# Attention scores turned onto the key side, with the row maximum entered as a contraction row and the sums formed by additions in PSUM

## The reference

```
xr   = x.reshape(B, C, S).transpose(0, 2, 1)
qkv  = (xr @ w_qkv + b_qkv).reshape(B, S, 8, 192);  q, k, v = split(qkv, 3)
attn = softmax(einsum('bihd,bjhd->bijh', q, k) * 64**-0.5, axis=2)
out  = einsum('bijh,bjhd->bihd', attn, v).reshape(B, S, 512) @ w_proj + b_proj
return out.transpose(0, 2, 1).reshape(x.shape) + x
```

## Time and profile before

| | us |
|---|---|
| median of 3 runs | 4386.79 (4386.68 to 4387.8) |
| span of the profiled execution | 4385.1 |
| TensorE busy, share | 4312.1, 98% |
| VectorE | 3439.8, 78% |
| ScalarE | 3020.3, 69% |
| GpSimd | 2179.6, 50% |

### The profile page before, as it was taken

How to read it: one execution, slowest core, us unless ns; L and a number is a source line. 1 busy time by engine, 2 the same in 40 slices (tenths; PEclk the granted TensorE clock), 3 DMA queues, 4 the chain that set the end, 5 groups by cost and what they waited for, 6 DMA issues and landing times.

```text
span 4385.1 us, 83037 instructions
## 1 busy us (share of the span) xinstructions
PE 4312.1 (98%) x28160; PEld 3820.6 (87%) x28160; DVE 3439.8 (78%) x5208; ACT 3020.3 (69%) x5271; POOL 2179.6 (50%) x1220
## 2 busy tenths in 40 slices
PE   8999999999999999999999999999999999999999
PEld 7888888888888888888888888888888888888887
DVE  7878878788787887878878788787887878878787
ACT  6767767677676776767767677676775767767675
POOL 4544544545454454544545445454454544545444
PEclk9999999999999999999999999999999999999999
DMA  2020120201202012021120201211111111111101
GB/s 85 16 64 25 32 62 18 64 23 32 62 18 64 24 31 61 21 61 25 30 61 24 61 23 30 62 28 56 25 35 54 30 54 25 43 46 32 54 16 49
DMA packets 100097, 178.23 MB, mean 41 GB/s; under 512 B 16544, under 2 KB 16672, under 8 KB 99616
## 3 DMA queue, kind: packets, MB, share of 16 engines
q1 hardware_dynamic: 99616, 172.10, 13.9%
HBM read 71.38 MB, written 33.55 MB: 24 GB/s over the span
## 4 chain that ended last, share of the span: by engine, by line
PE 89%; issue 4%; DVE 4%; ACT 3%; DMA 0%; SPq 0%; DVEq 0%; ACTq 0%; POOL 0%
PE ps_o L402 20%; PE turned L352 20%; PE scores L344 19%; PE ps_g L314 18%; PE ps_g L328 8%; PE ps_o L314 3%; DVE q_hl L611 1%; ACT probs L487 1%; ACT o L541 1%; DVE k_ll L611 1%; ACT pt_h L555 1%; DVE negmax L598 1%; DVE pt_l L670 1%; DVE pt_l L697 0%; DVE o L657 0%
## 5 line engine op out<-in xcount | busy, mean ns | idle before, releaser
L724 POOL TENSOR_TENSOR probs<-probs,rinv 128x1024 f32<-128x1024 f32 x1024 | 1939.0, 1894 | 2079.7 <-DVE rinv L603 2079.6
L555 ACT ACTIVATE pt_h<-turned 128x512 fp32r<-128x512 f32 x2048 | 1122.0, 596 | 924.8 <-PE turned L352 914.7
L598 DVE TENSOR_REDUCE negmax<-scores 128x1 f32<-128x1024 f32 x1024 | 1250.8, 1222 | 264.5 <-PE scores L344 221.5
L487 ACT ACTIVATE probs<-scores,negmax 128x1024 f32<-128x1024 f32 x1024 | 1145.3, 1118 | 290.2 <-DVE negmax L598 282.8
L670 DVE TENSOR_TENSOR pt_l<-turned,pt_h 128x512 fp32r<-128x512 f32 x2048 | 1310.6, 681 | 10.4 <-ACT pt_h L555 1.4
L352 PEld LDWEIGHTS turned<-idm,probs 128*128 128x128 f32 x8192 | 943.3, 140 | 230.7 <-DVE pt_l L670 89.0
L352 PE MATMUL turned<-idm,probs 128*128 128x128 f32 x8192 | 1088.2, 274 | 43.5 <-DVE pt_l L670 42.4
L402 PE MATMUL ps_o<-pt_h,v_hl 128*128 128x256 f32 x4096 | 1099.8, 302 | 2.7 <-DVE o L657 2.1
L402 PE MATMUL ps_o<-pt_l,v_hl 128*128 128x256 f32 x4096 | 1019.7, 282 | 0.0
L344 PE MATMUL scores<-k_ll,q_hl 128*128 128x512 f32 x2048 | 805.1, 393 | 0.0
L344 PE MATMUL scores<-k_hh,q_hl 128*128 128x512 f32 x2048 | 802.2, 392 | 0.9 <-DMA k_ll<-k_ll 0.9
(11 more groups left out here) (81 smaller groups left out, 4081.5 us busy)
## 6 DMA issues: line engine op xcount, KB each, us to landing
o<-x_in SPq DMA_DIRECT2D x130, 256.0 KB, 3.5
k_hh<-k_hh SPq DMA_DIRECT2D x256, 128.0 KB, 2.2
k_ll<-k_ll SPq DMA_DIRECT2D x256, 128.0 KB, 2.3
out<-o SPq DMA_DIRECT2D x128, 256.0 KB, 2.5
ring<-x_in SPq DMA_DIRECT2D x125, 256.0 KB, 2.9
o<-w_qkv_in SPq DMA_DIRECT2D x3, 768.0 KB, 6.2
o<-w_proj_in SPq DMA_DIRECT2D x1, 1024.0 KB, 5.4
probs<-w_qkv_in SPq DMA_DIRECT2D x1, 768.0 KB, 8.7
```

The lines of the kernel that those rows point to most:

```text
L487: nc.scalar.activation(probs[u % 2][:], scores[u % 2][:], ACT.Exp, bias=negmax[:, u % 2:u % 2 + 1], scale=1.0, accum_out=sums[:, u % 2:u % ...
L555: nc.scalar.activation(pt[0][:, u // 2 % 2, QT * f:QT * (f + 1), col:col + P], turned[fill % 2][:], ACT.Copy).then_inc(fill_high, 1)
L598: nc.vector.tensor_reduce(negmax[:, u % 2:u % 2 + 1], scores[u % 2][:], AXX, ALU.max, negate=True).then_inc(max_done, 1)
L724: nc.gpsimd.tensor_tensor(probs[u % 2][:], probs[u % 2][:], rinv[:, u % 2:u % 2 + 1].broadcast_to([P, S]), ALU.mult).then_inc(norm_done, 1)
```

## The change

- **Scores.** A unit is now 256 keys (two blocks of 128 on the partitions) against 512 queries of one head. Each block is two matmuls of 512 columns: `k1` (high part of k twice) with `q1` (high and low part of q), and `k2` (a row of ones, zeros, and the low part of k) with `q2` (the negated maxima as row 0, zeros, and the high part of q). So a block leaves PSUM as score minus maximum, already with the keys on the partitions, and nothing is transposed. The output half (512 queries) is complete after 4 units.
- **Maximum.** For 128 queries one pass over high k gives first scores (`first_scores`, two matmuls of 512 columns into `s1`). VectorE reduces them to `nm`, seven events ahead of use. Four columns of `nm` go to DRAM and come back as one row of `q2`.
- **Exponential.** ScalarE makes it twice per block: to `p` (fp32) and to `p_h` (rounded). GpSimd subtracts to `p_l`. TensorE multiplies V with `p_h` and `p_l`, 512 columns each.
- **Sums.** VectorE adds all `p` of a half into one PSUM bank (`acc`). Its high and low part are multiplied by a matrix of ones; row by row the sum goes to DRAM, to 64 partitions, through a reciprocal, back to DRAM and spread over 64 rows (`rinv`). GpSimd multiplies the output half with it.
- **q and k.** They are split at full 128 rows into one buffer `qk_h`, `qk_l`. At each head's start SP moves them with five transfers of 256 KB to `k1`, `q1`, `k2` of the next head, and half of `q2` by another of 128 KB. These wait for the last score product of the old head.
- **Weights.** The loading stage splits w_qkv and writes it to DRAM. Each head's 512 KB is loaded again in the loop (`wq`, two buffers), and V's half (`wv`, one buffer).
- **Order.** Every two units have one projection group, half in each (`GROUP`). The output projection of an image lies in the body of the next one, and a last body without new work drains. The bias of V is carried through w_proj into `bp` once.

In the diff, `at(per, i)` is the count of events at item i of this image, and `B.slot` numbers the uses of the three banks `st`.

```diff
-def score(u):
-    head, it = u // IT, u % IT
-    i = head % 2
-    for n in range(NH):
-        for e, kk in enumerate((k_hh, k_ll)):
-            last = nc.tensor.matmul(scores[u % 2][:, n * HALF:(n + 1) * HALF],
-                                    q_hl[i][:, it * P:(it + 1) * P],
-                                    kk[i][:, n * HALF:(n + 1) * HALF],
-                                    start=e == 0, stop=e == 1)
-    return last
-def turn(bank, blocks):
-    for j, blk in enumerate(blocks):
-        last = nc.tensor.transpose(turned[bank][:, j, :], blk, idm[:])
-    return last
...
-pe.wait_ge(norm_done, UNITS * b + (u + 1))
-        pe.wait_ge(v_low, VS * b + V0)
-    else:
-        pe.wait_ge(fill_low, FILLS * b + (fill - 1))
-    turn(fill % 2, [probs[u % 2][:, j * P:(j + 1) * P]
...
-                         ACT.Copy).then_inc(fill_high, 1)
-    fill += 1
-if more or u + 2 < UNITS:
...
-def normalise(u, unit):
-    pool.wait_ge(recip_done, unit + 1)
-    nc.gpsimd.tensor_tensor(probs[u % 2][:], probs[u % 2][:],
-                            rinv[:, u % 2:u % 2 + 1].broadcast_to([P, S]),
...
+GROUP = {0: ("v", 3), 6: ("out", -8), 8: ("out", -7), 14: ("out", -6), 16: ("out", -5),
+         22: ("v", 4), 24: ("v", 5), 30: ("v", 6), 32: ("v", 7),
+         38: ("out", -4), 40: ("out", -3), 46: ("out", -2), 48: ("out", -1),
+         54: ("v", 8), 56: ("v", 9), 62: ("v", 10)}
+for head in range(HEADS):
+    for n in range(NH):
+        GROUP[8 * head + 2 + 2 * n] = ("qk", 2 * (head + 2) + n)
+PER_BATCH = {"qk": 16, "v": 8, "out": 8}
...
+def move_head(head):
+    i = head % 2
+    for dst, src in ((k1[i][0:D, :], qk_h[D:P, :]), (q1[i][0:D, :], qk_h[0:D, :]),
+                     (k1[i][D:P, :], qk_h[D:P, :]), (q1[i][D:P, :], qk_l[0:D, :]),
+                     (k2[i][D:P, :], qk_l[D:P, :])):
+        sp.dma_start(dst.bitcast(f32), src.bitcast(f32)).then_inc(moved[i], 16)
+def fill_q2(head, n):
+    sp.dma_start(q2[D:P, cols(n)].bitcast(f32), q1[head % 2][0:D, cols(n)].bitcast(f32)
+                 ).then_inc(q2_filled[n], 16)
+def store_max(n):
+    sp.dma_start(max_d[n].rearrange("(t p) -> p t", p=P), nm[:, 4 * n:4 * n + 4].bitcast(f32),
+                 allow_slow_non_contiguous=True).then_inc(max_stored[n], 16)
...
+if u == 0 and B.now:
+    if (v := at(SLOTS, B.slot(U - 1, 1) + 1)) is not None:
+        sp.wait_ge(st_done, v)
+    fill_q2(h, 1)
+if u == 0 and B.on(h + 1, HEADS):
+    sp.wait_ge(l_done, at(2 * HEADS, 2 * (h + 1) + 2))
+    move_head(h + 1)
+if u == 1 and B.now:
+    sp.wait_ge(max_done, at(UNITS, 8 * h + 8))
+    store_max(1)
+if u == 2 and B.now:
+    sp.wait_ge(max_stored[1], at(16 * HEADS, 16 * (h + 1)))
+    load_max(1)
...
+if U % 4 == 2 and B.on(half := (U - 6) // 4, HALVES):
+    n = half % 2
+    sp.wait_ge(st_free, at(SLOTS, B.sum_slot(half) + 1))
+    sp.dma_start(sum_d[n:n + 1, :], sum_row[32 * n:32 * n + 1, :]).then_inc(row_stored[n], 16)
+if U % 4 == 3 and B.on(half := (U - 7) // 4, HALVES):
+    n = half % 2
+    sp.wait_ge(row_stored[n], at(16 * HEADS, 16 * (half // 2 + 1)))
+    sp.dma_start(s64[n][:], sum_d[n].rearrange("(p c) -> p c", p=D)).then_inc(s64_loaded[n], 16)
+if U % 4 == 1 and B.on(half := (U - 9) // 4, HALVES):
+    n = half % 2
+    sp.wait_ge(recip_done, at(HALVES, half + 1))
+    sp.dma_start(rinv_d[n].rearrange("(p c) -> p c", p=D), r64[n][:]).then_inc(recip_stored[n], 16)
+    sp.wait_ge(recip_stored[n], at(16 * HEADS, 16 * (half // 2 + 1)))
+    sp.dma_start(rinv[rows, n, :], rinv_d[n:n + 1, :].broadcast_to([D, HALF])
+                 ).then_inc(rinv_loaded[half % 4], 16)
...
+def first_scores(head, it):
+    for n in range(NH):
+        mm = nc.tensor.matmul(s1[:, cols(n)], q1[head % 2][:, it * P:(it + 1) * P],
+                              k1[head % 2][:, cols(n)], start=True, stop=True)
+    return mm
...
+if B.now:
+    if u % 4 == 0:
+        pe.wait_ge(q2_filled[n], at(16 * HEADS, 16 * (h + 1)))
+        pe.wait_ge(max_loaded[n], at(16 * HEADS, 16 * (h + 1)))
+    for e in range(2):
+        slot, keys = B.slot(U, e), slice((2 * (u % 4) + e) * P, (2 * (u % 4) + e + 1) * P)
+        if (v := at(SLOTS, slot - 2)) is not None:
+            pe.wait_ge(st_free, v)
+        nc.tensor.matmul(st[slot % RING][:], k1[i][:, keys], q1[i][:, cols(n)],
+                         start=True, stop=False)
+        nc.tensor.matmul(st[slot % RING][:], k2[i][:, keys], q2[:, cols(n)],
+                         start=False, stop=True).then_inc(st_done, 1)
+if B.on(event := U + MAX0, UNITS):
+    head, it = divmod(event, IT)
+    if it == 0:
+        pe.wait_ge(moved[head % 2], at(16 * MOVES * HEADS // 2, 16 * MOVES * (head // 2 + 1)))
+    pe.wait_ge(max_done, at(UNITS, event))
+    first_scores(head, it).then_inc(s1_done, 1)
+kind, i, e = B.group(U)
+if kind and e == 0 and held:
+    if held[0] == "qk":
+        pe.wait_ge(l_done, at(16, held[1] + 1))
...
+if U % 4 == 1 and B.on(half := (U - 5) // 4, HALVES):
+    slot = B.sum_slot(half)
+    pe.wait_ge(st_free, at(SLOTS, slot - 2))
+    pe.wait_ge(accl_done, at(HALVES, half + 1))
+    nc.tensor.matmul(st[slot % RING][:], ones[:], acc_h[:], start=True, stop=False)
+    nc.tensor.matmul(st[slot % RING][:], ones[:], acc_l[:], start=False, stop=True
+                     ).then_inc(st_done, 1)
+    if pair == 0 and (v := at(HALVES, unit // 4)) is not None:
+        pe.wait_ge(half_done, v)
+    for e in range(2):
+        slot = unit % 2 * 2 + e
+        values = v_hl[:, 2 * pair + e, V_SLOT[head], :]
+        pe.wait_ge(pl_done, at(2 * UNITS, 2 * unit + e + 1))
+        nc.tensor.matmul(ps_o[:], values, p_h[:, slot, :],
+                         start=pair == 0 and e == 0, stop=False)
+        mm = nc.tensor.matmul(ps_o[:], values, p_l[:, slot, :],
+                              start=False, stop=pair == 3 and e == 1)
+    mm.then_inc(pv_done, 1)
...
+if U % 4 == 1 and B.on(half := (U - 5) // 4, HALVES):
+    act.wait_ge(pv_done, at(UNITS, 4 * half + 4))
+    nc.scalar.copy(tmp[rows, half % 2, :], ps_o[other, :]).then_inc(half_moved, 1)
+if B.now:
+    for e in range(2):
+        slot, to = B.slot(U, e), U % 2 * 2 + e
+        act.wait_ge(st_done, at(SLOTS, slot + 1))
+        if (v := at(2 * UNITS, 2 * (U - 2) + e + 1)) is not None:
+            act.wait_ge(acc_done, v)
+            act.wait_ge(pl_done, v)
+        nc.scalar.activation(p[:, to, :], st[slot % RING][:], ACT.Exp)
+        if e == 0 and (v := at(UNITS, U - 1)) is not None:
+            act.wait_ge(pv_done, v)
+        nc.scalar.activation(p_h[:, to, :], st[slot % RING][:], ACT.Exp).then_inc(st_free, 1)
+kind, i, e = B.group(U)
+if kind == "qk" and e == 1:
+    head, n = divmod(i, 2)
+    qk_high(head, n, ps_g)
+if U % 4 == 0 and B.on(half := (U - 4) // 4, HALVES):
+    act.wait_ge(acc_done, at(2 * UNITS, 8 * half + 8))
+    nc.scalar.copy(acc_h[:], acc[:]).then_inc(acch_done, 1)
...
+def add_probs(B, unit, e):
+    probs = p[:, unit % 2 * 2 + e, :]
+    dve.wait_ge(st_free, B.at(SLOTS, B.slot(unit, e) + 1))
+    if unit % 4 == 0 and e == 0:
+        if (v := B.at(HALVES, unit // 4)) is not None:
+            dve.wait_ge(accl_done, v)
+        nc.vector.tensor_copy(acc[:], probs).then_inc(acc_done, 1)
+    else:
+        dve.wait_ge(acc_done, B.at(2 * UNITS, 2 * unit + e))
+        nc.vector.tensor_tensor(acc[:], acc[:], probs, ALU.add).then_inc(acc_done, 1)
+def maximum(it):
+    nc.vector.tensor_reduce(nm[:, it:it + 1], s1[:], AXX, ALU.max, negate=True).then_inc(max_done, 1)
...
+if U % 4 == 1 and B.on(half := (U - 5) // 4, HALVES):
+    rows, _ = half_rows(half)
+    dve.wait_ge(acch_done, at(HALVES, half + 1))
+    nc.vector.tensor_tensor(acc_l[:], acc[:], acc_h[:].bitcast(f32), ALU.subtract
+                            ).then_inc(accl_done, 1)
+    dve.wait_ge(half_moved, at(HALVES, half + 1))
+    nc.vector.tensor_tensor(tmp[rows, half % 2, :], ps_o[rows, :], tmp[rows, half % 2, :],
+                            ALU.add).then_inc(half_done, 1)
+if B.on(unit := U - 1, UNITS):
+    add_probs(B, unit, 0)
+if B.on(event := U + MAX0, UNITS):
+    head, it = divmod(event, IT)
+    if it % 4 == 0 and (v := at(16 * HEADS, 16 * head)) is not None:
+        dve.wait_ge(max_stored[it // 4], v)
+    dve.wait_ge(s1_done, at(UNITS, event + 2))
+    maximum(it)
+if B.on(unit := U - 1, UNITS):
+    add_probs(B, unit, 1)
+if U % 4 == 0 and B.on(half := (U - 8) // 4, HALVES):
+    n = half % 2
+    dve.wait_ge(s64_loaded[n], at(16 * HEADS, 16 * (half // 2 + 1)))
+    nc.vector.reciprocal(r64[n][:], s64[n][:]).then_inc(recip_done, 1)
+kind, i, e = B.group(U)
+if kind == "qk" and e == 1:
+    dve.wait_ge(h_done, at(16, i + 1))
+    qk_low(i // 2, i % 2, ps_g)
...
+if B.now:
+    for e in range(2):
+        to = U % 2 * 2 + e
+        pool.wait_ge(st_free, at(SLOTS, B.slot(U, e) + 1))
+        if e == 0 and (v := at(UNITS, U - 1)) is not None:
+            pool.wait_ge(pv_done, v)
+        nc.gpsimd.tensor_tensor(p_l[:, to, :], p[:, to, :], p_h[:, to, :].bitcast(f32),
```

(88 more changed lines are left out.)

825 lines of the change are left out of this document (364 added, 461 removed).

## The result

The changed kernel takes 4976.02 us (median of 4 runs, 4969.8 to 4982.6), the kernel before 4387.3 (4386.7 to 4389.6): ratio 1.134, 95% interval 1.133 to 1.136. It is slower by 589 us; 4117 had been forecast. The profiled execution spans 4974.0 us at a mean granted clock of 0.92.

What follows compares the result with a forecast made beforehand. TensorE's matmul issue rate was taken as the bound: 98 loading + 3854 for sixteen batches - 41 outside the loop + 41 tail = 3952, plus 114 moves, 25 accumulator chain, 24 restarts, 2 around the span: 4117 us, range 3970 to 4345.

Steps and rivals of the forecast that it cites:

- Maxima through DRAM: Store and reload of the maxima as one row: 4.1 us landing, hidden with 1.5 us in hand.
- far end: Bad case for the maxima's transfer: at twice 4.1 us, 2.6 us late 128 times, 330 us.
- Chain two: SP's moves of the next head's keys and queries: at 228 GB/s TensorE waits 0.9 us, 127 times, 114 us.
- The clock: TensorE's granted clock: stayed 1.00 despite short waits before, so no wait was priced with a slower clock.
- other restarts: Small TensorE waits: 24 us in all, a sixth of the 9.5 us per batch of before.
- TensorE's work: Matmuls: 240.9 us per batch, units of 3.63 and 4.08 us; batches of 246 to 252 us expected.
- An addition into the accumulator: VectorE's 128x512 additions into PSUM: 0.681 us each, 128 per batch.
- rival B: VectorE is the bound, 249 us per batch, 4210 us in all; chance 0.17.
- The loading: Start of the kernel, with split weights going through DRAM: 98 us until maxima are loaded (85 to 130).
- D: TensorE's 512-column products take 0.25 us instead of 0.227, adding 353 us, 4470 in all; chance 0.01.
- A: The moves of keys and queries land in time, without the 114 us wait: 4000 us; chance 0.22.
- Rival C: Head change costs more than the transposes: slower if moves run at 171 GB/s or less, late maxima adding 330; chance 0.07.

Runs made afterwards that it cites:

- e1: Changed kernel with the maxima stored in 16-byte pieces, the first score product taking every fourth query: 4432.28 us, ratio 1.010.
- e4: Changed kernel with the store of maxima kept, but SP not waiting for it and the row loaded from zeros: 4679.81 us, one run.
- e2: e1 with the first score product one unit later (MAX0 6 instead of 7): 4184.48 us, ratio 0.954.
- e3: Changed kernel with neither store nor load of the maxima, exponentials unshifted: 4397.41 us, ratio 1.002.
- e11: e3 with the first score product one unit later (MAX0 6 instead of 7): 4083.40 us, one run.
- e10: Changed kernel with only the first score product one unit later (MAX0 6 instead of 7): 5733.26 us, ratio 1.306.
- e6: e5 with the loops of all engines written out: 4071.36 us, ratio 0.928.
- e5: e2 with VectorE's loop over batches written out: 4100.45 us, ratio 0.934.
- e7: e5 with GpSimd computing only 8 of 512 columns of the low parts of the next image's x: 4060.43 us, one run.

## Why the prediction was wrong

**The step that failed is "Maxima through DRAM".** It took the store at 4.1 us, from the row of the biases, and called it hidden with 1.5 us in hand. The row was the wrong kind: a load of 512 small elements stood for a store of them. A store of a first half takes 9.0 us, 2.2 times that (8.5 even for the first one, with nearly nothing else on its way). For a second half the step had 7.5 us from issue to landing, queue included, and 11.4 passed. The text saw that the trace had no such store and named twice 4.1 as its far end, which was about the size for first halves. From 4976 to e1, 544 us.

What it made of that far end was wrong too: 330 us in TensorE's waits for the row. These waits are 54.4 us. The step looked only at who needs the row. It did not ask who is queued behind SP's wait at L262. For the first half that wait ends 0.7 us before the old head's last product (median; in 42 of 127 heads after it), and SP still has the row of the sums in front of the copy and the moves. So these go out 3.1 us late, and TensorE waits 543.5 us for them where 251.3 remain in e1. e4 shows that the queue is held even with no wait of SP for the store.

**Chain two was mis-sized.** TensorE's wait for the moves had been put at 0.9 us, 127 times, 114 us. In e1 it is 251.3 us in 126, 2.0 each. Six transfers of 1.44 MB: in e1 pass 3.6 us on average from the first issue to the last, and the last lands 5.5 later, 9.1 in all where 7.9 was the sum (the changed kernel has the same 9.1). Less the 1.6 fixed that is 1.44 / 7.5 = 192 GB/s, not 228. Removing the wait by one unit more brought 248 us (e1 to e2) and 295 (e3 to e11), about the measured waits of 251.3 and 261.8 and over twice 114. The Trainium skill (SBUF — State Buffer, Door 1: the DMA port swizzle) gives about 218 GB/s in the limit and 196 at 1 MiB for 64 partitions: the 192 of e1 lies below both and is closer to the 196 than to the 228 that I took, though the page's 196 is for one single transfer.

**The clock.** "I price no wait with a slower clock": with a wait of 0.9 a head that might have held, with these it didn't. The mean granted clock is 0.92 after, 0.89 in e10, 0.985 in e2 and 0.99 in e6. What it can have cost directly are the 235 us of e3 above that are not idle time; no run changes the clock alone.

**The turn of the loop and the x splits** stand in no step: 84 us and 29 (e5, e6), and 40 (e7). The 24 us for other restarts were too few.

**What held.** TensorE's work: units of 3.67 and 4.12 us in e2 where 3.63 and 4.08 were predicted, and 247 a batch in e6 against 240.9 and restarts ("246 to 252"). An addition into the accumulator takes 0.690 (0.681 predicted), and VectorE is nowhere the bound: rival B is out. The loading: the first score product with loaded maxima at 97.29 us, 98 predicted, but that is luck: the store in it took 8.5, and with the fast store of e2 the same product starts at 89.63. D is out too. A was wrong on the moves.

**Rival C** was the one that came true, in its place (the change of head) and sign. It was priced by the rate of the moves, with late maxima as an addition of 330 us; the store turned out to be the larger part, the moves' own rate the smaller one, and the store's lateness reached TensorE through the moves. Its chance of 0.07 rested on "small stores never seen" being one doubt among several, when it was a cost without any row at all.

Together, by medians: 4976.0, less 543.7 (pieces of 16 bytes), less 247.8 (a unit for the moves), less 84.0 (VectorE's turn), less 29.1 (the other turns) gives 4071.4 for e6. That lies 46 under the forecast, and e2, with its loops kept as in the kernel before, 67 over it: the idea was worth about what its TensorE sum said, and two transfers took it away.

## What to carry to other kernels

- Before something goes through DRAM in small pieces, look at how the pieces lie there. Making the four values on a partition neighbours (by choosing which queries a product takes) changed nothing else and was worth 544 us.
- A wait on an in-order queue costs whatever stands behind it. For each new wait list the next instructions of that queue and when each is wanted, also with the transfer at two or three times its guessed time; a cost without a row of its own kind deserves that.
- A buffer of time between two chains is shared: the same one unit gained 248 us where the store was fast and lost 757 where it was slow.
